# Eighteen weight places instead of eleven, last rows and down weights on ScalarE's queue, no holding operations

## The reference

```python
slot = flat * C + jnp.minimum(pos, C - 1)          # C = 96 slots per expert
buf = jnp.zeros((E * C, H), x.dtype).at[slot].set(x[tok]).reshape(E, C, H)
g = jnp.einsum('ech,emh->ecm', buf, Wg)            # E = 64, M = 176, H = 256
u = jnp.einsum('ech,emh->ecm', buf, Wu)
out = jnp.einsum('ecm,ehm->ech', jax.nn.silu(g) * u, Wd).reshape(E * C, H)
yk = out[slot].reshape(T, K, H)                    # K = 6 experts per token
y = jnp.sum(yk * topk_w[..., None].astype(yk.dtype), axis=1)
```

## Time and profile before

| | us |
|---|---|
| median of 3 runs | 1053.91 (1053.9 to 1055.69) |
| the profiled execution's own time | 1056.7 |
| its span, first to last instruction | 1055.0 |
| first matmul of expert 0 to that of expert 63 | 850.79 to 1009.92 |
| start of the last scatter | 1024.96 |

### The profile page before, as it was taken

How to read it: one execution, slowest core, us unless ns; L and a number is a source line. 1 busy time by engine, 2 the same in 40 slices (tenths; PEclk the granted TensorE clock), 3 DMA queues, 4 the chain that set the end, 5 groups by cost and what they waited for, 6 DMA issues and landing times. The chain is left out here.

```text
span 1055.0 us, 18375 instructions
## 1 busy us (share of the span) xinstructions
PE 984.8 (93%) x6301; PEld 876.3 (83%) x6301; DVE 681.9 (65%) x1815; ACT 585.3 (55%) x1093; POOL 405.9 (38%) x599
## 2 busy tenths in 40 slices
PE   4999999999999999999999999999989799998973
PEld 4799999999999999999999999999865466555642
DVE  3566667778778876877887686887568132222356
ACT  2566766766676667676666767666531034333420
POOL 3122223223224554322455442235524424555560
PEclk9899999999999999999999999999999999999985
DMA  9992000001000101100010012000015169999957
GB/s 352 334 330 69 0 0 1 1 2 56 1 1 18 43 32 38 56 2 1 17 42 28 23 43 93 9 7 11 16 43 153 37 170 293 289 291 281 256 88 239
DMA packets 65289, 99.31 MB, mean 94 GB/s; under 512 B 8271, under 2 KB 46426, under 8 KB 64824
## 3 DMA queue, kind: packets, MB, share of 16 engines
q1 hardware_dynamic: 41192, 69.19, 21.3%
q0 software_dynamic: 11808, 12.87, 6.0%
q10 hardware_dynamic: 12208, 16.21, 4.9%
HBM read 66.11 MB, written 38.86 MB: 99 GB/s over the span
## 5 line engine op out<-in xcount | busy, mean ns | idle before, releaser
L442 POOL TENSOR_TENSOR holdp<-neghalf 128x1 f32<-128x1 f32 x145 | 31.5, 218 | 465.2 <-ACT prob L605 241.0
L599 ACT ACTIVATE prob<-ps,rn 128x512 f32<-128x512 f32 (+3 forms) x256 | 121.0, 526 | 124.2 <-PE ps L1317 116.5
L1291 PE MATMUL ps<-wh,hth 128*128 128x384 f32 x512 | 178.5, 349 | 5.2 <-DVE htl L791 3.1
L1291 PE MATMUL ps<-wh,htl 128*128 128x384 f32 x512 | 173.0, 338 | 0.0
L1291 PE MATMUL ps<-wl,hth 128*128 128x384 f32 x512 | 172.9, 338 | 0.0
L839 DVE TENSOR_REDUCE ss<-arena 128x8 f32<-128x1024 f32 x64 | 78.1, 1220 | 128.6 <-ACT arena L575 128.4
L1344 PE MATMUL ps<-vx,prob 128*128 128x129 f32 (+1 forms) x1280 | 153.5, 274 | 0.4 <-POOL prob L490 0.4
L1344 PEld LDWEIGHTS ps<-vx,prob 128*128 128x128 f32 x1280 | 148.6, 191 | 0.7 <-POOL prob L490 0.7
L575 ACT ACTIVATE arena<-ps 128x1024 f32<-128x1024 f32 x64 | 65.7, 1026 | 124.0 <-PE ps L1291 124.0
L554 POOL DMA_INDIRECT acc<-wos,arena x64 | 92.5, 1446 | 100.4 <-ACT wos L719 83.6
L496 POOL DMA_INDIRECT slot_rows<-pay,arena x96 | 97.6, 1017 | 42.9 <-issue 24.6
(11 more groups left out here) (194 smaller groups left out, 2192.7 us busy)
## 6 DMA issues: line engine op xcount, KB each, us to landing
wge<-in_wgu SPq DMA_DIRECT2D x30, 352.0 KB
slot_rows<-pay SPq DMA_DIRECT2D x1, 6456.0 KB, 35.3
acc<-pay SPq DMA_DIRECT2D x3, 2048.0 KB, 19.0
arena<-slot_rows ACTq DMA_DIRECT2D x56, 100.9 KB
warena<-in_wqkv SPq DMA_DIRECT2D x1, 4992.0 KB, 20.3
prob<-in_wgu SPq DMA_DIRECT2D x12, 352.0 KB
arena<-in_wgu SPq DMA_DIRECT2D x12, 352.0 KB
warena<-acc SPq DMA_DIRECT2D x8, 512.0 KB, 8.6
```

Of the source, the lines that this page charges most:

```text
L599: act_(prob[:, OFF[j]:OFF[j] + w], sflat[:, OFF[j]:OFF[j] + w], ACT.Tanh, scale=rn[:, bass.ds(head(n), 1), TT + j:TT + j + 1].squeeze(1)). ...
L1291: last = mm(ps[:, i, 0:3 * DH], hp[:, k, i * P:(i + 1) * P], wp[:, k, :], start=(k == 0 and m == 0), stop=(k == KC - 1 and m == 2))
```

## The change

1. The ring has 18 places. The memory comes from freeing the tiles that only attention uses (`heads.close()`), and from a new order of places.
2. SP loads the places 5 to 17 in pieces, each behind the wait that says its memory is free: gate and up of 5 and 6 at the start, the others from the last qkv of attention on; the piece that stood after x2 (13 DMAs) is gone.
3. The last rows of experts 0 to 7 are copied straight from `lrow` into `xg` ahead of the table wait; after it the other 95 slot rows are loaded, and the last rows of experts 8 to 63 go to `slot_rows` behind the first of these. The wait for `last_out` moves to ACT, ahead of `e_rows(8)`.
4. ACT, not SP, issues the last row of each result, three periods later in program order, straight into `o95` in SBUF; the tensor `last_rows` and its load are gone. `e_rows` comes ahead of `e_down`.
5. All holding operations go (145 on POOL, 40 on DVE), and POOL's loop over periods 2 to 11 of batch 0 is written out.

```diff
-RING = 11
+RING = 18
-        wgus += [gu_place(prob[:, u * GW:(u + 1) * GW]) for u in range(2)]
-        wgus += [gu_place(arena2[:, late + u * GW:late + (u + 1) * GW]) for u in range(2)]
-        wgus += [gu_place(warena[:, tail + u * GW:tail + (u + 1) * GW]) for u in range(2)]
+        heads.close()
...
+        wgus += [gu_place(arena2[:, rat[0] + u * GW:rat[0] + (u + 1) * GW]) for u in range(2)]
+        wgus += [gu_place(m[:, 0:GW]) for m in late_gu]
+        wgus += [gu_place(warena[:, tail + u * GW:tail + (u + 1) * GW]) for u in range(2)]
+        wgus += [gu_place(prob[:, u * GW:(u + 1) * GW]) for u in range(2)]
+        wgus += [gu_place(arena2[:, late + u * GW:late + (u + 1) * GW]) for u in range(2)]
+        wgus += [gu_place(rcur[:].rearrange("p c d -> p (c d)")[:, 0:GW])]
@@ SP: start, after the rows of batch 0
+            gate_ups(range(5, 7))
             sp.sem_inc(s["tab_free"], 1)
@@ SP: last batch
+            sp.wait_ge(s["qkv_rdy"], B * H)
+            gate_ups(range(7, 13))
+            sp.wait_ge(s["wol_rdy"], cnt(B - 1, H - 2))
+            downs(range(4, 8))
+            sp.wait_ge(s["s_rdy"], 3 * B * H)
+            downs(range(8, 12))
+            sp.wait_ge(s["o_rdy"], B * H)
+            gate_ups(range(13, 15))
+            downs(range(12, 15))
             sp.wait_ge(s["tabw"], 16 * TT * K * (B - 1))
             sp.sem_inc(s["tab_free"], 1)
+            sp.wait_ge(s["y_rdy"], 2 * B * H)
+            downs(range(15, 17))
+            sp.wait_ge(s["x2_rdy"], 2 * B + 1)
+            gate_ups(range(15, 17))
+            downs(range(17, 18))
             sp.wait_ge(s["hmod"], 2 * B)
...
-            sp.wait_ge(s["o_rdy"], B * H)
-            sp.wait_ge(s["y_rdy"], 2 * B * H)
-            sp.wait_ge(s["x2_rdy"], 2 * B + 1)
-            for u in range(EARLY, RING):
-                if u >= GEARLY:
-                    sp.dma_start(wgus[u], wgu[u]).then_inc(w_in[u], 16)
-                sp.dma_start(wds[u], wd[u]).then_inc(w_in[u], 16)
+            gate_ups(range(17, 18))
 
             sp.wait_ge(s["last_gat"], 16)
             sp.wait_ge(s["tables"], 16 * (1 + NACC))
+            for e in range(XR):
+                sp.dma_start(xg[C - 1:C, e, :], lrow[e:e + 1, :]).then_inc(xg_in[e], 16)
             sp.wait_ge(s["tabw"], 16 * NT * K)
-            sp.dma_start(buf_d.rearrange("(e s) c -> e s c", e=E)[:, C - 1, :], lrow[:]).then_inc(s["last_out"], 16)
-            sp.wait_ge(s["last_out"], 16)
             for e in range(XR):
-                sp.dma_start(xg[0:C, e, :], buf_d[e * C:(e + 1) * C, :]).then_inc(xg_in[e], 16)
+                sp.dma_start(xg[0:C - 1, e, :], buf_d[e * C:(e + 1) * C - 1, :]).then_inc(xg_in[e], 16)
+                if e == 0:
+                    sp.dma_start(buf_d.rearrange("(e s) c -> e s c", e=E)[XR:E, C - 1, :], lrow[XR:E, :]).then_inc(s["last_out"], 16)
@@ SP: expert loop and tail
-                if e >= 2:
-                    last_row(e - 2)
                 if e == ACUT + 4:
                     third_sum()
+            for a in range(2):
+                sp.wait_ge(ys[a], adds(a, E))
             for u in range(ORING):
                 sp.wait_ge(o95s[u], 16 * len(range(u, E, ORING)))
-            sp.dma_start(o95, o95_d).then_inc(s["o95_ld"], 16)
-            for a in range(2):
-                sp.wait_ge(ys[a], adds(a, E))
@@ POOL (and the like at four other places, and at nine on DVE)
                 pool.wait_ge(s["ss_rdy"], cnt(b, n))
-                hold(2)
@@ ACT: experts
+            def e_last_row(e):
+
+                a.wait_ge(s["orow_rdy"], e + 1)
+                a.dma_start(o95[e:e + 1, :], orow[e % ORING][C - 1:C, :]).then_inc(o95s[e % ORING], 16)
...
+                if n == XR:
+                    a.wait_ge(s["last_out"], 16)
                 a.wait_ge(s["wcol_rdy"], 2 * (n - XR) + 2)
...
                 e_silu(e, base)
+                if e >= 3:
+                    e_last_row(e - 3)
                 if not (isinstance(base, int) and base + e < 2):
                     e_orow(e - 2, base) if e >= 2 or isinstance(base, int) else e_orow(e - 2 + XR, base - XR)
+                if XR <= e + LEAD < E:
+                    e_rows(e + LEAD)
                 if e >= 2 and e - 2 + RING < E:
                     e_down(e - 2)
-                if XR <= e + LEAD < E:
-                    e_rows(e + LEAD)
...
+            e_last_row(E - 3)
             e_orow(E - 2, 0)
+            e_last_row(E - 2)
             e_orow(E - 1, 0)
+            e_last_row(E - 1)
@@ DVE: before the last rows are scaled
-            v.wait_ge(s["o95_ld"], 16)
+            for u in range(ORING):
+                v.wait_ge(o95s[u], 16 * len(range(u, E, ORING)))
```

More of the change, by code:

```diff
@@ L249, in build, with hb, gu_place, wd_place @@
         iotat1 = sb("iotat1", [P, NT])
+        heads = ctx.enter_context(ExitStack())
+        def hb(name, shape):
+            return heads.enter_context(nc.sbuf_tensor(name, shape, F32R))
+        hth = hb("hth", [P, KC, T])
+        htl = hb("htl", [P, KC, T])
+        wh = hb("wh", [P, KC, 3 * DH])
+        wl = hb("wl", [P, KC, 3 * DH])
+        qth = hb("qth", [P, T])
+        qtl = hb("qtl", [P, T])
+        kth = hb("kth", [P, T])
+        ktl = hb("ktl", [P, T])
+        oth = hb("oth", [P, T])
+        otl = hb("otl", [P, T])
+        heads.close()
+        late_gu = [sb("late_h", [P, KC * T]), sb("late_l", [P, KC * T]), sb("late_wh", [P, KC * 3 * DH]), sb("late_wl", [P, KC * 3 * DH])]
+        late_wd = [sb(f"late_t{i}", [P, T]) for i in range(6)]
+        def gu_place(v):
+            return v.rearrange("p (k m) -> p k m", k=KC)
+        def wd_place(v):
+            return v.rearrange("p (m d) -> p m d", m=2)
+        GW, DW, tail = 2 * KC * M, 2 * D, half + 4096
+        wgus = [wge[:, u] for u in range(GEARLY)]
+        wgus += [gu_place(arena2[:, rat[0] + u * GW:rat[0] + (u + 1) * GW]) for u in range(2)]
[4 more added lines that the diff above has]
+        wgus += [gu_place(rcur[:].rearrange("p c d -> p (c d)")[:, 0:GW])]
+        wds = [wde[:, u] for u in range(EARLY)]
+        wds += [wos[0:MR, c:c + 2, :] for c in (4, 6, 11, 13)]
+        wds += [wd_place(m[0:MR, :]) for m in late_wd[0:4]]
+        wds += [wd_place(vx[0:MR, (u + 1) * DW:(u + 2) * DW]) for u in range(3)]
+        wds += [wd_place(m[0:MR, :]) for m in late_wd[4:6]]
+        wds += [wd_place(arena2[0:MR, late + 2 * GW:late + 2 * GW + DW])]
+        assert late + 2 * GW + DW <= 4096 and rat[0] + 2 * GW <= 8704 and len(wgus) == RING and len(wds) == RING
         names = """ld_x0 ld_wq0 ld_x ld_c ld_wmod ld_wmod2 ld_small ld_wqkv ld_wo ld_gate ld_sh consts fills tables
@@ L331, in _, with gate_ups, downs @@
             sp.dma_start(gates[:], gate).then_inc(s["ld_gate"], 16)
-            for u in range(GEARLY):
-                sp.dma_start(wgus[u], wgu[u]).then_inc(w_in[u], 16)
-            for u in range(EARLY):
-                sp.dma_start(wds[u], wd[u]).then_inc(w_in[u], 16)
+            def gate_ups(us):
+                for u in us:
+                    sp.dma_start(wgus[u], wgu[u]).then_inc(w_in[u], 16)
+            def downs(us):
+                for u in us:
+                    sp.dma_start(wds[u], wd[u]).then_inc(w_in[u], 16)
+            gate_ups(range(GEARLY))
+            downs(range(EARLY))
             sp.wait_ge(s["fills"], 2)
@@ L524, in _ @@
                 period(0, p)
-            with pool.Fori(2, SIDE) as p:
+            for p in range(2, SIDE):
                 period(0, p)
@@ L756, in _ @@
             tt, ts, cp = nc.vector.tensor_tensor, nc.vector.tensor_scalar, nc.vector.tensor_copy
-            def hold(c):
-                nc.vector.memset(holdv[:, c:c + 1], 0.0)
             def ln_stats(l, b):
@@ L821, in h2_modulated @@
                 v.wait_ge(s["tab_free"], b + 1)
-                hold(7)
                 for i in range(TT):
@@ L906, in taken @@
             def taken(b, c, out, v8, src):
-                hold(c)
                 for i in range(TT):
@@ L1109, in x_last @@
                 v.wait_ge(s["x2_rdy"], 2 * b + 3)
-                hold(0)
             def shared_half(b, q):
```

43 lines of the change are left out of this document (3 added, 40 removed).

## The result

The changed kernel's median is 1048.24 us (1045.77 to 1049.95, 7 runs), that of the kernel before beside it 1053.91 us (1051.43 to 1056.99, 7 runs): ratio 0.9941, 95% interval 0.992 to 0.9961. The forecast was 1047.8 us, faster. Measured again beside the last experiments, the ratio was 0.993 (0.9911 to 0.9949). The profiled execution took 1048.57 us, its span is 1046.7 against 1055.0 before: 8.3 us less in the profile, 5.7 in the medians.

What follows compares the result with a forecast made beforehand. DMA was taken to be full among the experts, with the scatter queue's lag ending the kernel. Scatter tail 5.3 plus holds 0.8 made 6.1 us off the median 1053.9, giving 1047.8 us; range 1039 to 1052.5.

Steps and rivals of the forecast that it cites:

- The limit: Among the experts DMA is full at 292 GB/s; the scatter queue's lag, not the weights, ends the kernel.
- From there to the end all is fixed: Kernel's end: after the last scatter lands, accumulator loads and DVE's sums follow in fixed time.
- The scatter tail, 5.3 us: Last experts: with 18 ring places the last scatter starts at 1019.7 instead of 1024.96; bounds 1.0 to 9.7 us.
- PE's gaps behind expert 46, 1.0 us: Experts 46 to 63: PE's idle gaps of 1.0 us vanish, so expert 63 is reached at 1008.9.
- PE's gaps before expert 46, 0: Experts 12 to 46: the 9.7 us of PE gaps stay, gain 0; at most 9.7 if late weights caused them.
- The lag, 15.0 to 10.8: Last gate matmul to last scatter: lag shrinks after expert 46, partly returning with the third accumulator's load.
- Holding operations, 0.8 us (0 to 1.2): Removed holds gain 0.4 us at the start, 0.4 in the last routing, 0 in attention, where PE is full.
- Preloads, slot rows, last rows on ScalarE, 0: Attention, before expert 0 and among the experts: these moved loads and issues are hidden and change the time by 0.
- The shared expert's gap (16%): Rival, 16%: PE's unexplained gap before expert 0 closes, 6.8 us more gained, 1041 us.
- weights bound the experts (7%): Rival, 7%: total DMA traffic among the experts sets the pace, so 13.4 us go, 1040 us.
- the lag stays (13%): Rival, 13%: scatters at the end keep 8 us turns or the earlier accumulator load cancels the gain, 1052.5 us.
- ScalarE's queue (11%): Rival, 11%: among the experts, last rows land late on ACT's queue and slow the kernel to 1056 to 1068 us.

Runs made afterwards that it cites:

- t_noload: The changed kernel without the 2 MB load of the third accumulator, DVE's operations on that memory kept: 1046.74 us, ratio 0.9935 to the kernel before.
- ring_only: The kernel before with only the ring of 18 places and its preloads put in: 1041.29 us, ratio 0.9965 to the kernel before.
- noholds_only: The kernel before with only the holding operations taken out, POOL's loop written out: 1043.15 us, ratio 0.9977 to the kernel before.
- ring_noholds: The changed kernel with last rows back on SP and the old slot rows; ring of 18, no holds: 1038.28 us, ratio 0.9928 to the kernel before.
- u_ring11: The changed kernel with the ring and its preloads cut back to 11 places: 1054.87 us, ratio 1.0007 to the kernel before.
- late_third: The changed kernel with DVE's six operations on the third accumulator moved behind the last six experts: 1049.62 us, ratio 0.9945 to the kernel before.
- group 1: Runs on chip 3, each taking one part of the changed kernel back; the kernel before takes 1053.49 us there.
- group 2: Runs on chip 13 with ring, missing holds or both, without the two queue edits; the kernel before takes 1045.41 us there.
- u_lastrow_sp: The changed kernel with last rows back on SP's queue, written to memory and loaded once at the end: 1048.79 us, ratio 0.9959 to the kernel before.
- u_slots: The changed kernel with last rows copied after the table wait, then 96-row loads for experts 0 to 7: 1046.60 us, ratio 0.9935 to the kernel before.
- after2: The changed kernel itself, measured again as base of the last group: 1046.99 us, ratio 0.993 to the kernel before.

## Why the prediction was right, and where it was not

**The limit.** Right for this change. The scatters' lag is what the ring moves: 15.0, 15.7 and 14.9 us with eleven places, 11.7 to 12.4 in all with eighteen that load the third accumulator. "From there to the end all is fixed" did not hold: from the last scatter to the first sum it is 9.7 us before, 9.0 now, and 11.1 in t_noload, where POOL took longer over this scatter beside DVE's operations. The last weight issue came at 962.8, not 966 or 967, since PE was ahead by then.

**The scatter tail, 5.3 us.** Right in sum: like against like, the ring gives 3.7 us (ring_only) and 4.9 (noholds_only to ring_noholds), and 6.6 beside the queue edits (u_ring11 against the changed kernel, medians of different groups). The 3.7 has an interval of 1.4 to 5.9. Its parts were less exact.
- PE's gaps behind expert 46, 1.0 us: not seen in the profiled pair, where 46 to 63 takes 41.58 and 41.64. From 50 to 63 the size is right: 30.86 us in every kernel of 18 places and 31.56 to 31.98 with 11, which is 0.7 to 1.1. In the changed kernel the gaps that were left stood at experts 48 and before, so PE was at full pace later than forecast.
- PE's gaps before expert 46, 0: in the two profiles 4.5 us went. This step failed, in part: from 0 to 50 the three profiles with eleven places give 122.9 to 127.6 us, those with eighteen (spread apart) 121.4 to 125.1, means of 125.7 and 123.6. Some 2 us may be the ring's; the kernel before's 127.57 is the slowest of all, and the forecast took it for typical. The spread within each kind is larger than the difference, so this stays unsettled.
- The lag, 15.0 to 10.8: it fell to 12.0. By expert 50 the part that could go was gone, as forecast. But what cannot go is 8.5 us (experts 50 to 53, and up to 60 in t_noload) and 7.90 for the last expert of t_noload, where the forecast set 6.4 by an estimate: 1.5 too low. Then the third accumulator's load brought 4.1 us back; 4.4 was forecast, as 5.7 lost, 3.0 regained and 1.7 for the last two turns. Scatter 53 to 54 is 5.72 us instead of 2.39, 3.3 late, where 3.7 was set, and expert 55 adds 0.7, where some 2 were set. What did not come is the regain of 0.6 us in each of five turns: turns on one accumulator are 4.7 us, not 4.19, while POOL's scatter takes 1.9 us and not 1.41 beside DVE's sums. The 4.19 of the earlier trace rows was read where no such sum lay, and in late_third, with the sums moved away, the turns are 4.13 to 4.24. So 4.1 agrees with 4.4 because the loss and the regain were both set too large.

**Holding operations, 0.8 us (0 to 1.2).** The term that was mis-sized: 2.4 us alone, 3.0 beside the ring (1041.29 to 1038.28), 4.4 put back. "In attention PE is full, so 0" is the step that failed. PE is busy 77.11 of 80 us, so it has idle time in every stretch, and a chain through POOL shows in it: each of 64 rounds grows by 0.04 us. The 2.4 us have an interval of 0.3 to 4.5; that attention gets shorter by 2.2 to 2.5 us is the firmer reading. About a sixth of one hold's 0.26 us reached PE in a round. In the profiled pair the gap hid this, by chance: before stood at 849.69, while holds put back gave 851.73 and kernels without them 846.47 to 849.87.

**Preloads, slot rows, last rows on ScalarE, 0.** Right within what can be told, for the whole change: ring_noholds, without the last two, has 0.9928, the changed kernel 0.9941 and 0.993. Where the ring or the holds are as before, the pairs of group 1 and group 2 leave room for a cost of 2 to 3 us. The down weights, which the title names too, were on ScalarE's queue in the kernel before. ScalarE's issue takes 0.52 us where 0.44 was set, and nobody waited for it.

The Trainium skill's rule on a queue's order ("DMA: Bandwidth & Descriptors", Queues, rings and completion order) may well hold for these rows. It is a rule on the order in which descriptors are consumed, and the section says that a later one may finish its write before an earlier one. No wait shows either: nobody waited 10 us for a last row.

**Sum and rivals.** 6.1 us were forecast and 5.7 measured. That is closer than the working, and in part luck: holds were too small by about 2, the ring too large by 1.6 (3.7 measured alone for 5.3, though 5.3 lies in its interval), and in the profiled pair PE's pace gave 4.4 us of which the forecast had 1.0. The shared expert's gap (16%) did not close through this change. That it is fragile was right, and so was its price: 6.8 forecast, 7.8 when half the last batch's transfers go, some 8 on the chip where no profile has it. The text named their end as what stood near DVE's release and counted the unchanged transfers against this rival; both were the right thing to look at. That weights bound the experts (7%) fell: the lag moved with the ring, and 13.4 us did not go. That the lag stays (13%) fell, though its reason, DVE's work beside POOL's, is part of what held it at 12 us: late_third had regained 1.8 us from expert 55 to 60, the changed kernel 0.1. ScalarE's queue (11%) fell with u_lastrow_sp.

No version beat the changed kernel by more than can be told: u_slots (1046.60) and ring_noholds, which is simpler, are level with it.

## What to carry to other kernels

An engine that is busy 96% of the time isn't full: a small serial step removed from each of many rounds comes through in part, so count rounds times a fraction of it before writing 0. The pace of a chain of transfers is to be read where its neighbours will be those of the new place, since the same scatter took 1.41 us alone and 1.9 to 3.3 beside another engine's large operations. Two errors that cancel look like a good forecast, so its terms are to be checked one by one. And a gain in one stage is to be taken to the next wait: the 3.9 us of lag that went with a load came back as 0.25 us.

## What was not expected of the hardware

- Kernels with all table transfers have a gap of some 8 us in the shared expert on two chips (first transposes at 846.5 to 851.7) and none on a third (837.6 to 840.9), though the transfers end at 831 to 834.5 on all three. The kernel before is 1053.5 and 1054.3 us on the ones and 1045.4 on the other.
- Where it appears, it goes with the last twelve of POOL's small table transfers, and the granted clock is at its lower level behind it (0.50 for 10 us in after2).
- A scatter's time on POOL goes from 1.41 to as much as 3.29 us beside DVE's operations on 128x1024 f32.
